# A two-dimensional spectral kernel: constants as weights along w, turns through DRAM and half-channel passes

## The chip, the cores and the metric

The kernel runs on one core of one Trainium2 chip. The metric is the device time of one execution in microseconds (us), the median of several runs. Engines are named as in the profile: PE (TensorE) multiplies, DVE (VectorE) and ACT (ScalarE) copy results out of PSUM and do the elementwise work, POOL (GpSimd) and SP (SyncE) issue DMAs. PEld is PE's load of weights.

## The reference

Four spectral layers follow one another on x of 2 x 64 x 64 x 384 in fp32 (batch, h, w, channels). Layers 0, 2 and 3 have this form:

```python
xs = jnp.fft.rfft2(x, axes=(1, 2))                 # 64 x 33 modes
o1r = relu(xr @ w1[0] - xi @ w1[1] + b1[0])        # 8 blocks of 48 channels
o1i = relu(xi @ w1[0] + xr @ w1[1] + b1[1])
o2r = o1r @ w2[0] - o1i @ w2[1] + b2[0]
o2i = o1i @ w2[0] + o1r @ w2[1] + b2[1]
out = jnp.fft.irfft2(softshrink(o2r) + 1j * softshrink(o2i)) + x
```

Layer 1 has a Hartley transform over the batch, h, w and channels in place of the FFT, the same kind of block product on all 64 by the first 33 of its modes (with the mirrored array beside it), and adds its result to its input too. Between layers nothing but this addition touches the array in space, so the kernel stays in the space of modes from the first layer to the last.

## The kernel before, in words

Work is cut into units. `order()` writes all of them out in one list, and every engine walks that list in order. A unit fills one of four PSUM units of two banks on PE, then ACT and DVE empty it; PE waits before unit n until unit n-4 is empty (`take`). Keys name the stage, the image and the place.

**First part, per image** (2 images, i). `S1` transforms along w: the pixels of two rows of h (128 partitions) by 128 channels are the weights, and the constant `dft_w`, which holds the two rows apart with zeros, streams (132 columns, L623). `T1` turns each of 33 modes and 3 channel tiles with a transpose (L645). Then come 20 rounds, one for each step: a step is 6 or 7 modes of w (`GROUPS`) by a pair of the 8 channel blocks. A round holds `S2` (transform along h, L657), `TA` of step n-4 (transposes back, L688), `S3` of step n-1 and `S4` of step n-2 (the two block products, L669 and L678). `S3` uses 48 of 64 rows in the two row halves, `S4` the two 64-column halves. On DVE `S4` is shrunk (L1087) and added to the modes (L1073 or L1076); POOL stores the sum in the DRAM array `spectrum`. After the 20 rounds comes the inverse, only to get the flipped array that layer 1 wants: `5A` along h with the modes as weights (L704), `2A` transposes (L715), `6A` along w (L725), then a store to `flipped`. Image 1 begins after that.

**Middle part** (10 items of modes and image): `CF`, `H1`, `H2`, `CI` do layer 1 (L747 to L784), from `spectrum`, its channel-mirrored copy `mirrored` (made by DMA, L480) and `flipped`. The result goes to `update` and `update_mirrored`.

**Last part, per image**: 20 rounds plus 3 of `3L2`, `3L3`, `4L2`, `4L3`, `TC`: two layers' products in the same lines L669 and L678, and the transposes L688. DVE joins the loaded update to step n+2 in between. Then `5C` (L704), `2C` (L715) and `6C`: PSUM is split into a high and a low fp32r part on ACT and DVE (L1276) and three one-pass products of 512 columns give the output (L736). Image 1 follows.

S1, for one of these:

```python
for k in range(min(2 * S1_BANK, HP - 2 * S1_BANK * u)):
    at = k // S1_BANK * BANK + k % S1_BANK * n
    mm = nc.tensor.matmul(bank[:, at:at + n], X[:, 2 * S1_BANK * u + k, t * P:(t + 1) * P], dft_w,
                          start=True, stop=True)
```

SP's queue issues loads and the mirror copies, POOL's the stores, each in its own order; a DMA behind a wait on SP is late with all that follows.

## Time and profile before

| | |
|---|---|
| median of 3 runs | 1116.82 us (1116.59 to 1116.85) |
| the profiled execution | 1116.76 us, span of the core 1114.9 us, mean granted clock 0.979 |
| PE, DVE, ACT, POOL busy | 1059.5, 570.9, 513.4, 107.9 us |
| share of PE in the chain of waits | 88% |
| moved by DMA | 117.94 MB, mean 106 GB/s |

Busy time is that of instructions on the engine. An fp32 matmul stands as two records, one after the other; a transpose as one. The chain of waits is the work that ended last, followed back from the end; in order of time it says which stage the kernel stands in. The granted clock is 1 at 2.4 GHz.

### The profile page before, as it was taken

To read this page: it belongs to the slowest core of one execution; us is meant where nothing else is said; L and a number is where in the kernel's file an instruction comes from. 1 tells how busy PE (TensorE), PEld (TensorE's weight loads), DVE (VectorE), ACT (ScalarE), POOL (GpSimd) and SP (SyncE) were. 2 spreads that over 40 slices of the span, in tenths; PEclk is the share of its full clock that TensorE was granted. 3 is DMA by queue.
4 is the path that set the end of the run, shared out by engine and by line. 5 is a ranking of instruction groups with operands and counts; after the bars stand their busy time and mean duration, and the time that the engine had idled before them with its cause. 6 is when DMAs were issued, how large, how long until landed. Compare 5 with 4: busy or idle time off the path is not lost.

```text
span 1114.9 us, 15851 instructions
## 1 busy us (share of the span) xinstructions
PE 1059.5 (95%) x6238; PEld 657.1 (59%) x6238; DVE 570.9 (51%) x893; ACT 513.4 (46%) x783; POOL 107.9 (10%) x160
## 2 busy tenths in 40 slices
PE   5899999999999999999999998899998989999896
PEld 5865569997555895444444444244446954444495
DVE  2645565344555552451424222477775567777645
ACT  2355553345555332422233231266665546666544
POOL 0011220000112100001111112100000120000003
PEclk9899999999999999999999998699999989999999
DMA  9713331100333595445345632543330184330016
GB/s 307 261 30 83 97 101 44 79 40 25 83 87 100 137 270 161 77 112 112 108 98 151 123 107 73 153 112 86 86 100 14 57 226 105 89 86 22 2 39 188
DMA packets 108058, 117.94 MB, mean 106 GB/s; under 512 B 69302, under 2 KB 93478, under 8 KB 107218
## 3 DMA queue, kind: packets, MB, share of 16 engines
q1 hardware_dynamic: 84626, 68.91, 24.4%
q0 software_dynamic: 22048, 45.99, 13.8%
q10 hardware_dynamic: 1312, 2.03, 0.6%
q8 instruction: 51, 0.84, 0.3%
q14 instruction: 21, 0.17, 0.1%
HBM read 77.41 MB, written 52.25 MB: 116 GB/s over the span
## 4 chain that ended last, share of the span: by engine, by line
PE 88%; DVE 5%; issue 3%; ACT 2%; DMA 1%; POOL 0%; SPq 0%; ACTq 0%; DVEq 0%
PE psum L678 16%; PE psum L669 15%; PE psum L784 8%; PE psum L747 8%; PE psum L704 8%; PE psum L657 6%; PE psum L761 5%; PE psum L688 4%; PE psum L623 4%; PE psum L725 4%; PE psum L715 4%; PE psum L736 3%; PE psum L772 3%; PE psum L645 2%; DVE RA L1087 1%
## 5 line engine op out<-in xcount | busy, mean ns | idle before, releaser
L1087 DVE SCALAR_TENSOR_TENSOR RA<-psum,RA 112x896 f32<-112x896 f32 (+1 forms) x120 | 124.3, 1036 | 196.7 <-ACT RA L922 196.7
L1049 DVE COPY RD<-psum 128x396 f32<-128x396 f32 (+5 forms) x110 | 73.1, 667 | 175.5 <-PE psum L747 91.1
L922 ACT ACTIVATE RA<-psum,small 112x896 f32<-112x896 f32 (+1 forms) x120 | 115.7, 964 | 82.3 <-PE psum L678 81.3
L678 PE MATMUL psum<-RA,RW 112*64 112x448 f32 (+1 forms) x640 | 135.7, 546 | 10.2 <-ACT RA L913 5.4
L899 ACT ACTIVATE RD<-psum 128x396 f32<-128x396 f32 (+7 forms) x106 | 60.8, 574 | 156.5 <-PE psum L747 67.1
L913 ACT ACTIVATE RA<-psum,RW 112x448 f32<-112x448 f32 (+1 forms) x160 | 89.2, 609 | 91.4 <-PE psum L669 91.4
L899 ACT ACTIVATE RB<-psum 128x512 f32<-128x512 f32 (+1 forms) x128 | 73.1, 571 | 104.4 <-PE psum L704 69.0
L1049 DVE COPY RB<-psum 128x512 f32<-128x512 f32 (+1 forms) x130 | 84.7, 653 | 70.7 <-PE psum L704 53.4
L704 PE MATMUL psum<-const,RD 128*128 128x128 f32 (+1 forms) x792 | 93.5, 279 | 4.9 <-DVE RD L1049 3.5
L678 PEld LDWEIGHTS psum<-RA,RW 112*64 112x64 f32 x640 | 40.3, 139 | 96.6 <-issue 67.5
L704 PEld LDWEIGHTS psum<-const,RD 128*128 128x128 f32 x792 | 91.5, 195 | 8.4 <-DVE RD L1049 3.9
L784 PE MATMUL psum<-RB,RD 112*128 112x448 f32 (+1 forms) x240 | 92.1, 537 | 3.1 <-DVE RB L1238 3.1
L747 PE MATMUL psum<-RX,RD 128*112 128x448 f32 (+1 forms) x240 | 89.9, 525 | 0.0
L1073 DVE TENSOR_TENSOR RX<-RX,RA 112x768 f32<-112x768 f32 (+2 forms) x80 | 80.7, 1009 | 1.4
L669 PE MATMUL psum<-RX,RW 48*112 48x448 f32 (+1 forms) x320 | 71.2, 566 | 4.4 <-DVE RX L1076 2.3
L784 PEld LDWEIGHTS psum<-RB,RD 112*128 112x128 f32 x240 | 46.3, 197 | 47.1 <-issue 36.0
L657 PEld LDWEIGHTS psum<-const,RB 128*112 128x112 f32 x528 | 59.7, 177 | 24.2 <-ACT RA L913 21.5
L899 ACT ACTIVATE RA<-psum 112x896 f32<-112x896 f32 (+2 forms) x64 | 44.3, 693 | 55.4 <-PE psum L725 29.0
L747 PEld LDWEIGHTS psum<-RX,RD 128*112 128x112 f32 x240 | 40.9, 177 | 47.2 <-issue 33.8
L678 PE MATMUL psum<-RA,RB 112*64 112x448 f32 (+1 forms) x320 | 64.0, 520 | 5.0 <-ACT RA L913 5.0
L657 PE MATMUL psum<-const,RB 128*112 128x128 f32 x528 | 67.1, 279 | 0.0
L669 PE MATMUL psum<-RA,RW 48*112 48x448 f32 (+1 forms) x320 | 67.0, 537 | 0.0
(91 smaller groups left out, 1329.7 us busy)
## 6 DMA issues: line engine op xcount, KB each, us to landing
out<-RB POOLq DMA_DIRECT2D x24, 512.0 KB, 3.8
RX<-x SPq DMA_DIRECT2D x10, 1152.0 KB, 13.5
spectrum<-RA POOLq DMA_DIRECT2D x48, 168.0 KB, 2.8
RX<-spectrum SPq DMA_DIRECT2D x48, 168.0 KB, 3.3
flipped<-RA POOLq DMA_DIRECT2D x6, 1056.0 KB, 4.8
spectrum<-RA POOLq DMA_DIRECT2D x32, 144.0 KB, 2.6
RX<-spectrum SPq DMA_DIRECT2D x32, 144.0 KB, 2.9
mirrored<-spectrum SPq DMA_DIRECT2D x6, 672.0 KB
```

What stands on the lines that cost most here:

```text
L657: mm = nc.tensor.matmul(bank[0:ROWS, k * P:(k + 1) * P], Bpair[:, k0 + k, g], dft_h, start=True, stop=True)
L669: mm = nc.tensor.matmul(dst, w3[layer][rows, a, g], src[rows, :, a], start=a == 0, stop=a == 1)
L678: mm = nc.tensor.matmul(bank[b * HALF:(b + 1) * HALF, a * BANK:a * BANK + nk * H], w4[layer][0:ROWS, g, b, a], hidden(slot)[0:ROWS, b * N: ...
L704: mm = nc.tensor.matmul(bank[:, at:at + n], D[:, k, t * P:(t + 1) * P], rhs, start=True, stop=True)
L747: mm = nc.tensor.matmul(bank[0:ROWS, half * BANK:half * BANK + n], fwd_c_view[:, t, 2 * h + half], y(q, 1 + 2 * b)[:, t], start=t == 0, st ...
L784: mm = nc.tensor.matmul(bank[:, half * BANK:half * BANK + n], inv_c_view[0:ROWS, g, t * P:(t + 1) * P], s_sum[b][0:ROWS, g, 0:n], start=g ...
L899: return nc.scalar.activation(dst, src, ACT.Copy)
L913: done = nc.scalar.activation(hidden(slot)[0:ROWS, b * N:b * N + nk * H], banks(key)[0:ROWS, b, 0:nk * H], ACT.Relu, bias=bias[layer][0:RO ...
L922: nc.scalar.activation(dst, src, ACT.Relu, bias=minus_lambda_l0 if key[0] == "S4" else minus_lambda).then_inc(act_emptied, 1)
L1049: return nc.vector.tensor_copy(dst, src)
L1073: last = nc.vector.tensor_tensor(m[:, :, k], m[:, :, k], src[:, :, k], ALU.add)
L1087: nc.vector.scalar_tensor_tensor(out=dst, in0=src, scalar=LAMBDA / 64 if key[0] == "S4" else LAMBDA, in1=dst, op0=ALU.add, op1=ALU.min).th ...
```

## The change

1. **Passes.** Images go through in four passes p of 192 channels (image p // 2, half p % 2). Steps are numbered s = 0 to 39 over both images, 10 to a pass; e = s // 2 numbers the 20 groups of modes. One list of rounds r runs over all 40 steps, in the first part as in the last: no pass ends before the next begins.
2. **Along w.** `S1` has the constant as weights (64 x 64) and x as the streaming side: four matmuls of 384 columns, one in each quarter of the array. `6C` is built alike, with plain fp32 and no split; so the `2C` units, L1276 and `inv_w_parts` go.
3. **Turns.** `T1`, `2A` and `2C` go. SP stores the transform along w to the DRAM array `rows_along_w` and loads it back with h on the partitions (`load_bm`); the inverse along h goes to `rows_along_h` (`store_turned`) and comes back with w's modes on the partitions (`load_g`).
4. **Along h, inverse.** `5A` and `5C` have the constant as weights and stream two modes of 192 channels.
5. `6A` works on 96 channels at a time. Preparing layer 1's operands on DVE is spread over steps 2 to 7. The `CF` units of the first two items go ahead of the `6A` units of the last pass.

On PE and in the plan:

```diff
--- before.py
+++ after.py
-            def s1(i, u, t):
-                key = ("S1", i, u, t)
-                if t == 0:
-                    pe.wait_ge(x_loaded[u], 16 * (i + 1))
+            def s1(p, v):
+                key, k = ("S1", p, v), v // 2
+                if v % 2 == 0:
+                    pe.wait_ge(x_loaded[k], 32 * (p + 1))
                 bank = take(key)
-                n = 4 * KW
-                for k in range(min(2 * S1_BANK, HP - 2 * S1_BANK * u)):
-                    at = k // S1_BANK * BANK + k % S1_BANK * n
-                    mm = nc.tensor.matmul(bank[:, at:at + n], X[:, 2 * S1_BANK * u + k, t * P:(t + 1) * P], dft_w,
-                                          start=True, stop=True)
+                n = 2 * PASS_C
+                for to in range(2):
+                    at = (to * X_HP // 2 + v % 2 * 2) * PASS_C
+                    for j in range(2):
+                        rows = slice(j * HALF, (j + 1) * HALF)
+                        mm = nc.tensor.matmul(bank[to * HALF:(to + 1) * HALF, j * BANK:j * BANK + n], dft_w[rows],
+                                              X(k)[rows, at:at + n], start=True, stop=True)
                 mm.then_inc(filled, 1)
...
-            def t1(i, v):
-                key = ("T1", i, v)
-                if v == 0:
-                    for t in range(NT):
-                        for u in (S1_UNITS - 2, S1_UNITS - 1):
-                            wait_emptied(pe, ("S1", i, u, t))
+            def s2(s):
+                key, e = ("S2", s), s // PASS_PAIRS
+                _, g, k0, nk = step_of(s)
                 bank = take(key)
-                for k in range(2 * v, min(2 * v + 2, KW)):
-                    for t in range(NT):
-                        at = (k % 2) * BANK + t * P
-                        mm = nc.tensor.transpose(bank[:, at:at + P], A(t)[:, :, k], identity)
-                mm.then_inc(filled, 1)
-
-            def s2(i, n):
-                key = ("S2", i, n)
-                q, g, k0, nk = step_of(n)
-                bank = take(key)
-                if g == 0:
-                    last = (k0 + nk - 1) // 2
-                    for v in (last - 1, last):
-                        wait_emptied(pe, ("T1", i, v))
+                if s == 0:
+                    pe.wait_ge(consts_loaded, 16)
+                if s % PASS_PAIRS == 0:
+                    wait_bm_loaded(pe, e)
+                cols = slice(g % PASS_PAIRS * ROWS, (g % PASS_PAIRS + 1) * ROWS)
                 for k in range(nk):
-                    mm = nc.tensor.matmul(bank[0:ROWS, k * P:(k + 1) * P], Bpair[:, k0 + k, g], dft_h,
+                    rows = slice(0, H) if k0 + k in (0, KW - 1) else slice(0, P)
+                    mm = nc.tensor.matmul(bank[0:ROWS, k * P:(k + 1) * P], Bm(e)[rows, k, cols], dft_h[rows],
                                           start=True, stop=True)
                 mm.then_inc(filled, 1)
...
-            def s5(key, matrix, turned):
-                _, i, t, u = key
-                if t == 0:
-                    modes = [k for m in inverse_banks(u) for k in bank_modes(m)]
-                    n = max(n for n in range(STEPS) if step_of(n)[1] == PAIRS - 1 and step_of(n)[2] <= max(modes))
-                    wait_emptied(pe, (turned, i, n))
+            def s5(key, matrix, stage, first):
+                _, e, part = key
+                if part == 0:
+                    for s in (PASS_PAIRS * e, PASS_PAIRS * e + 1):
+                        wait_emptied(pe, (stage, s))
                 bank = take(key)
-                for half, m in enumerate(inverse_banks(u)):
-                    at = half * BANK
-                    for k in bank_modes(m):
-                        rhs = matrix[:, 2 * H:3 * H] if k in (0, KW - 1) else matrix[:, 0:2 * H]
-                        n = rhs.shape[1]
-                        mm = nc.tensor.matmul(bank[:, at:at + n], D[:, k, t * P:(t + 1) * P], rhs, start=True, stop=True)
-                        at += n
+                for half in range(2):
+                    lo, hi = bank_modes(e, part, half)
+                    n = (hi - lo) * PASS_C
+                    dst = bank[:, half * BANK:half * BANK + n].rearrange("p (k c) -> p k c", c=PASS_C)
+                    mm = nc.tensor.matmul(dst, matrix, D(first + e)[:, lo:hi], start=True, stop=True)
                 mm.then_inc(filled, 1)
 
-            def t2(key, s5_stage):
-                _, i, t, v = key
-                if v == 0:
-                    for u in range(INV_UNITS):
-                        wait_emptied(pe, (s5_stage, i, t, u))
+            def s6a(key):
+                _, p, g, v = key
+                if g == 0 and v == 0:
+                    pe.wait_ge(g_loaded[p % 2], 32 * (p // 2 + 1))
                 bank = take(key)
-                for k in range(HP_UNIT):
-                    mm = nc.tensor.transpose(bank[:, k * P:(k + 1) * P], E(t)[:, :, v * HP_UNIT + k], identity)
-                mm.then_inc(filled, 1)
-
-            def s6a(key):
-                _, i, t, v = key
-                bank = take(key)
-                wait_emptied(pe, ("2A", i, t, v))
-                n = 2 * KW
-                for k in range(HP_UNIT):
-                    at = k // (HP_UNIT // 2) * BANK + k % (HP_UNIT // 2) * n
-                    mm = nc.tensor.matmul(bank[:, at:at + n], G(t, v)[:, k * P:(k + 1) * P], inv_w_flip,
+                n, cols = 2 * KW, slice(g * PASS_C // 2, (g + 1) * PASS_C // 2)
+                for k in range(FLIP_HP):
+                    at = k // (FLIP_HP // 2) * BANK + k % (FLIP_HP // 2) * n
+                    mm = nc.tensor.matmul(bank[0:PASS_C // 2, at:at + n], G(p)[:, v * FLIP_HP + k, cols], inv_w_flip,
                                           start=True, stop=True)
                 mm.then_inc(filled, 1)
 
             def s6c(key):
-                _, i, t, v = key
+                _, p, v = key
+                if v == 0:
+                    pe.wait_ge(g_loaded[p % 2], 32 * ((PASSES + p) // 2 + 1))
                 bank = take(key)
-                wait_emptied(pe, ("2C", i, t, v))
-                for half in range(2):
-                    cols = slice(half * BANK, (half + 1) * BANK)
-                    for n, (matrix, g) in enumerate(((0, 0), (1, 0), (0, 1))):
-                        mm = nc.tensor.matmul(bank[:, cols], inv_w_parts[:, matrix], split(t, v)[g][:, cols],
-                                              start=n == 0, stop=n == 2)
+                n, k = 2 * PASS_C, v // 2
+                for to in range(2):
+                    h = k * X_HP + to * X_HP // 2 + v % 2 * 2
+                    for j in range(2):
+                        rows = slice(j * HALF, (j + 1) * HALF)
+                        dst = bank[to * HALF:(to + 1) * HALF, j * BANK:j * BANK + n].rearrange("p (h c) -> p h c", c=PASS_C)
+                        mm = nc.tensor.matmul(dst, inv_w[rows], G(p)[rows, h:h + 2], start=True, stop=True)
                 mm.then_inc(filled, 1)
 
```

The first part's and last part's rounds, and SP's queue:

```diff
+def first_transform_round(p):
+    return 3 if p == 1 else 10 * p - 8
+
+
+def flip_round(p):
+    return 10 * p + 17
+
+
+def last_inverse_round(p):
+    return 10 * p + 16
+
+
+def order():
+    o = [("S1", 0, v) for v in range(S1_UNITS)]
+    for r in range(A_ROUNDS):
+        if r < ALL_STEPS:
+            o += [("S2", r)]
+        if 0 <= r - 4 < ALL_STEPS:
+            o += [("TA", r - 4)]
+        for p in range(1, PASSES):
+            if 0 <= r - first_transform_round(p) < X_PARTS:
+                o += [("S1", p, 2 * (r - first_transform_round(p)))]
+        for p in range(PASSES - 1):
+            if 0 <= r - flip_round(p) < FLIP_UNITS:
+                o += [("6A", p, 0, r - flip_round(p))]
+        if 0 <= r - 1 < ALL_STEPS:
+            o += [("S3", r - 1)]
+        if 0 <= r - 6 < 2 * ALL_GROUPS:
+            o += [("5A", (r - 6) // 2, (r - 6) % 2)]
+        if 0 <= r - 2 < ALL_STEPS:
+            o += [("S4", r - 2)]
+        for p in range(1, PASSES):
+            if 0 <= r - first_transform_round(p) < X_PARTS:
+                o += [("S1", p, 2 * (r - first_transform_round(p)) + 1)]
+        for p in range(PASSES - 1):
+            if 0 <= r - flip_round(p) < FLIP_UNITS:
+                o += [("6A", p, 1, r - flip_round(p))]
+        if r == PREP_ROUND:
...
+    for r in range(C_ROUNDS):
+        if r < ALL_STEPS:
+            o += [("3L2", r)]
+        if 0 <= r - L3_LAG - 3 < 2 * ALL_GROUPS:
+            o += [("5C", (r - L3_LAG - 3) // 2, (r - L3_LAG - 3) % 2)]
+        if 0 <= r - L3_LAG < ALL_STEPS:
+            o += [("3L3", r - L3_LAG)]
+        if r < ALL_STEPS:
+            o += [("4L2", r)]
+        for p in range(PASSES - 1):
+            if 0 <= r - last_inverse_round(p) < S1_UNITS:
+                o += [("6C", p, r - last_inverse_round(p))]
+        if 0 <= r - L3_LAG < ALL_STEPS:
+            o += [("4L3", r - L3_LAG)]
+        if 0 <= r - L3_LAG - 1 < ALL_STEPS:
+            o += [("TC", r - L3_LAG - 1)]
+    o += [("6C", PASSES - 1, v) for v in range(S1_UNITS)]
...
+            def store_stage(p, k):
+                wait_emptied(sp, ("S1", p, 2 * k))
+                wait_emptied(sp, ("S1", p, 2 * k + 1))
...
+                for to in range(2):
+                    at = (2 * k + to) * n
+                    sp.dma_start(dst[:, :, at:at + n], src[to * HALF:(to + 1) * HALF]
+                                 ).then_inc(stage_stored[(p * X_PARTS + k) % STAGE_SLOTS], 16)
+
+            def load_bm(e):
+                p, q, k0, nk = group_of(e)
+                if q == 0:
+                    for k in range(1, X_PARTS):
+                        wait_stage_stored(sp, p, k)
+                loaded = bm_loaded[e % BM_SLOTS]
+                src = rows_along_w[p].rearrange("q h r -> h q r")
+                n_re = nk - (q == PASS_GROUPS - 1)
...
+                sp.dma_start(Bm(e)[0:H, 0:n_re], src[:, 2 * k0:2 * (k0 + n_re):2]).then_inc(loaded, 16)
+                sp.dma_start(Bm(e)[H:P, skip:n_re], src[:, 2 * (k0 + skip) + 1:2 * (k0 + n_re):2]).then_inc(loaded, 16)
...
+            def store_turned(e):
+                p, q, k0, nk = group_of(e)
...
+                sp.dma_start(dst[:, 2 * k0:2 * (k0 + n_re):2], turned(e)[0:H, 0:n_re]).then_inc(stored, 16)
+                sp.dma_start(dst[:, 2 * (k0 + skip) + 1:2 * (k0 + n_re):2], turned(e)[H:P, skip:n_re]).then_inc(stored, 16)
...
+            def load_g(p):
+                for e in (PASS_GROUPS * (p + 1) - 2, PASS_GROUPS * (p + 1) - 1):
+                    wait_turned_stored(sp, e)
...
+                for j in range(2):
+                    sp.dma_start(G(p)[j * Q:(j + 1) * Q], rows_along_h[p, :, j * HP:(j + 1) * HP]
+                                 ).then_inc(g_loaded[p % 2], 16)
...
+            for r in range(A_ROUNDS):
+                for p in range(1, PASSES):
+                    k = r - first_transform_round(p)
+                    if 0 <= k < X_PARTS:
+                        store_stage(p, k)
+                        if p + 1 < PASSES:
+                            load_x(p + 1, k)
+                e = (r + 4) // 2
+                if r % 2 == 0 and BM_SLOTS <= e < ALL_GROUPS:
+                    wait_filled(sp, ("S2", 2 * (e - BM_SLOTS) + 1))
+                    load_bm(e)
+                if r % 2 == 1 and 0 <= (r - 7) // 2 < ALL_GROUPS:
+                    e = (r - 7) // 2
+                    for part in range(2):
+                        wait_emptied(sp, ("5A", e, part))
+                    store_turned(e)
+                for p in range(PASSES - 1):
+                    if r == 10 * p + 16:
+                        load_g(p)
+                for i in range(B):
+                    if r % 2 == 1 and 0 <= r - i * STEPS - 15 < 2 * PASS_GROUPS:
+                        mirror(i, (r - i * STEPS - 15) // 2)
```

**PE's order, the end of the first inverse.** Before, PE's rows at the end of image 0 (L704 is 5A, L688 TA, L715 2A, L725 6A, L623 S1):

```order
L688 MATMUL psum<-const,RA 128x112 x6
L678 MATMUL psum<-RA,RW 64x384 x4
L704 MATMUL psum<-const,RD 128x128 x8
L688 MATMUL psum<-const,RA 128x112 x6
L704 MATMUL psum<-const,RD 128x128 x8
```

And in the change, a round with transform units of pass 2 and the next ones (L825 is S2, L856 TA, L802 S1, L837 S3, L870 5A, L846 S4):

```order
L825 MATMUL psum<-const,RX 112x128 x7
L856 MATMUL psum<-const,RA 128x112 x7
L802 MATMUL psum<-RX,const 64x384 x4
L837 MATMUL psum<-RA,RW 112x448 x4
L870 MATMUL psum<-RD,const 128x192 x2
L846 MATMUL psum<-RA,RW 64x448 x4
L802 MATMUL psum<-RX,const 64x384 x4
```

The inverse along h (5A) and the transform of a later pass (S1) have moved into the rounds, between units that split the array.

**SP's order in the change, from the end of round 15 to the array of pass 0** (L529 is a staged store of pass 2, L517 x of pass 3, L552 to L555 the turned group 4, L591 a mirror copy, L541 and L542 a load for S2, L569 the array for 6A of pass 0):

```order
L529 DMA rows_along_w<-RX 128x1x896 [waits vec_emptied,act_emptied]
L529 DMA rows_along_w<-RX 128x1x896
L517 DMA RX<-x 64x8x192 x2
L552 DMA rows_along_h<-RD 64x5x192 [waits vec_emptied,act_emptied]
L553 DMA rows_along_h<-RD 64x5x192
L555 DMA rows_along_h<-RD 64x192
L591 DMA mirrored<-spectrum 7x384x64 [waits modes_stored3,modes_stored4,modes_stored1,modes_stored0]
L541 DMA RX<-rows_along_w 64x7x224 [waits stage_stored1,stage_stored2,stage_stored0,filled]
L542 DMA RX<-rows_along_w 64x6x224
L569 DMA RG<-rows_along_h 64x6144 [waits prep_stored,turned_stored0,turned_stored1]
L569 DMA RG<-rows_along_h 64x6144
```

All of these but the mirror copy and x are new, and the array for 6A comes last of them.

**The end of PE's list in the change** (L896 is 6C):

```order
L856 MATMUL psum<-const,RX 128x112 x6
L870 MATMUL psum<-RD,const 128x384 x2
L896 MATMUL psum<-RG,const 64x384 x4
L870 MATMUL psum<-RD,const 128x192 x2
L896 MATMUL psum<-RG,const 64x384 x32
```

The last eight units of 6C (x32) stand behind the last unit of 5C, with nothing between.

## Rows read from the trace of the kernel before

**Rows 1.** The page: busy time, share of the span and instructions by engine

```profile
PE 1059.5 (95%) x6238; PEld 657.1 (59%) x6238; DVE 570.9 (51%) x893; ACT 513.4 (46%) x783; POOL 107.9 (10%) x160
```

**Rows 2.** Chain of waits in order of time, first part: start us, us, what

```profile
45.13 12.41 PE psum L645 x99
57.54 3.06 PE psum L657 x28
...
101.05 1.71 PE psum L657 x14
...
106.78 1.71 PE psum L657 x14
...
171.75 11.43 PE psum L704 x100
183.18 3.60 PE psum L715 x32
...
194.14 1.74 PE psum L725 x16
...
222.57 21.67 PE psum L623 x192
```

**Rows 3.** The same view, middle and last part

```profile
559.46 4.05 PE psum L747 x12
...
891.75 1.40 PE psum L736 x6
...
939.67 0.82 PE psum L688 x7
...
946.85 0.82 PE psum L688 x7
```

**Rows 4.** Timeline of PE: start us, us, line, operation, out<-in, count [idle before]

```profile
171.75 10.48 PE L704 MATMUL psum<-const,RD 128*128 128x128 f32 x92 [1.73 <-DVE RD L1049]
...
818.87 1.51 PE L678 MATMUL psum<-RA,RW 112*64 112x384 f32 x8 [0.28 <-DVE RA L1087]
820.21 1.46 PE L678 MATMUL psum<-RA,RB 112*64 112x384 f32 x8
821.60 0.79 PE L688 MATMUL psum<-const,RX 112*128 112x112 f32 x6
822.33 1.55 PE L669 MATMUL psum<-RX,RW 48*112 48x384 f32 x8
...
854.01 0.74 PE L688 MATMUL psum<-const,RX 112*128 112x112 f32 x6
854.59 1.96 PE L704 MATMUL psum<-const,RD 128*128 128x128 f32 x16
...
857.87 11.43 PE L704 MATMUL psum<-const,RD 128*128 128x128 f32 x100 [0.74 <-ACT RD L899]
...
907.35 2.28 PE L669 MATMUL psum<-RX,RW 48*112 48x448 f32 x8 [2.26 <-DVE RX L1076]
```

**Rows 5.** Groups by line and form: count, busy us, mean ns, idle before

```profile
L704 PEld LDWEIGHTS psum<-const,RD 128*128 128x128 f32 x792 | 91.5, 195 | 8.4 <-DVE RD L1049 3.9 <-ACT RD L899 1.9 <-DVE RA L1087 1.2
L657 PEld LDWEIGHTS psum<-const,RB 128*112 128x112 f32 x528 | 59.7, 177 | 24.2 <-ACT RA L913 21.5 <-issue 2.7
L1049 DVE COPY RB<-psum 128x384 f32<-128x384 f32 x34 | 18.7, 555 | 7.9 <-PE psum L645 7.9
```

**Rows 6.** Stretches (engines busy, PEclk, DMA share, GB/s) and a DMA issue

```profile
57.50:172.00 114.50, 112.77 (x751) 68.48 (x750) 61.20 (x104) 60.47 (x83) 22.52 (x45) 1.00 0.32 81
375.00:400.00 25.00, 25.00 (x222) 25.00 (x222) 10.52 (x16) 9.06 (x16) 0.00 (x0) 0.98 0.92 217
400.00:425.00 25.00, 25.00 (x220) 24.53 (x220) 15.10 (x22) 8.47 (x18) 1.11 (x2) 1.00 0.84 263
700.00:725.00 25.00, 21.07 (x68) 7.35 (x70) 11.56 (x37) 8.16 (x12) 3.49 (x3) 0.66 0.56 165
...
spectrum<-RA POOLq DMA_DIRECT2D x48, 168.0 KB, 2.8
```

938 lines of the change are left out of this document (496 added, 442 removed).

## The prediction

> **What bounds the kernel now.** I read the page first. PE is busy for 1059.5 of 1114.9 us, and nothing else is above 51% [rows 1]. So a change pays if it takes matmuls away or fills PE's 55 us of idleness; what it gives VectorE, ScalarE or the DMA queues costs only where PE comes to wait for it. The chain of waits in order of time gives every stage its length: each fp32 matmul is two records there, so x192 is 96 matmuls. In the first part [rows 2] a step of the mode rounds takes 5.73 us (101.05 to 106.78) and the stages along w and the inverse stand apart from the rounds. In the last part [rows 3] a round takes 7.18 us (939.67 to 946.85). The timeline [rows 4] prices matmuls that share the array, and the lines by form [rows 5] the weight loads. The stretches and DMA issues [rows 6] say what a turn through DRAM costs. The sum is made against the profiled execution, 1116.8 us with its 1.9 us around the span; the median of the runs is the same.
>
> **Matmul work taken out.** From the two chains [rows 2, 3]: the transform along w, 21.67 us per image, 43.3; its transposes, 12.41 each, 24.8; the inverse along h, 11.43 us per 100 records for 792 of them, 90.5; the 192 transposes of each inverse, 3.60 us per 32 records for 384 in all, 43.2; the flipped inverse along w, 1.74 per 16 for 384, 41.8; the last inverse, 24 units of 1.40, 33.6. Together 277.
>
> **Matmul work put in.** (a) The transform along w and the last inverse become 32 units each of four fp32 matmuls of 384 columns, one in each array quarter, so 8 records a unit. No row shows four quarters at once. Two 64-column halves at once take 1.34 us for 8 records of 384 columns (818.87 to 820.21) [rows 4], and the whole array takes 4.05 us for 12 [rows 3], 2.7 us for 8: a half doubles the rate and nothing of it is lost. Bounds for a unit are thus 0.70 us (doubled again) and 1.39 us (halves only; the spacing of 820.21 to 821.60). I take 0.70, because both row halves and column halves pair up fully in this kernel: 64 x 0.70 = 45 us. (b) The inverse along h gets the constant as its weights and 160 matmuls of 384 or 192 columns instead of 396 of at most 128: 208 records at 4.05/12 = 0.34 and 112 at some 0.18 give 90 us, the same as before. Fewer weight loads gain nothing, since streaming already set the pace. (c) The flipped inverse goes from 192 to 256 matmuls of 66 columns. They are bound by the load of the weights: 0.109 us a record is twice what 66 columns stream in. The weights have 96 columns instead of 128, and loads shrink with columns (195 against 177 ns for 128 and 112) [rows 5]. Between 0.082 and 0.109 us a record I take 0.082: 42 us. (d) Switching between whole and split array: six transposes before another whole-array matmul take 0.58 us (854.01 to 854.59), before a split one 0.73 (821.60 to 822.33) [rows 4]. The 80 inverse units now stand between row-split and column-split products, 0.15 us each, and the quarter units add about 0.05 to 0.1 each: 16 us. Together 193, and the net is **277 - 193 = 84 us less**.
>
> The Trainium skill (TensorEngine Tiling (Array Packing), § Key Properties) says that four 64x64 tiles run independently, and that changing the tiling mode drains the engine. By the first a unit takes 0.70 us as in my sum. By the second each switch would cost more than my row shows; the trace agrees that a switch costs something, 0.15 us.
>
> **Evacuation.** A quarter unit is copied out by two engines, 384 columns each. VectorE takes 555 ns for such a copy [rows 5], less than the 0.70 us of the unit, and two such units share a round with others; VectorE's 61 us in the 114.5 us of the first rounds [rows 6] leave room. I cost it at nothing in the first part. In the last part a round puts seven units through four PSUM units where five went before, and the copy of a last-inverse unit stands behind shrink, join and add; PE needs that PSUM unit four units later. Without that cover it is up to 1 us a round; I take 0.1, 4 us in all.
>
> **Turns through DRAM: the new waits.** At full share the queues move 263/0.84 = 313 GB/s, and a single 168 KB store lands after 2.8 us, so some 2.2 us are latency [rows 6]. Per pass of 192 channels an array for the inverse along w is 3.15 MB, 10.1 us. PE reaches that inverse (6A) about one and a half to two rounds after the last 5A unit of the pass, which is 9 to 11 us later, while on SP's queue stand, for pass 0: the last staged store 2.9, the next part of x 2.5, the turned store 2.2, the mirror copy 3.2, a load for the forward transform 2.5, then the array 10.1 and latency 2.2, and 2 for the mode stores beside them: 27.7 us against 9.3, so PE stands for **18 us**. For pass 1 there is no x and no mirror: 22 against 9.3, **13**. Pass 2: 20 against 11, **9**. Pass 3: 18 against the 7 us of three CF units, **11**. Each stop also lets the clock fall (the granted clock was 0.66 in the 25 us after the quiet stretch at 700 us [rows 6]): 2 us each, 8. Together **59 us**. The mirror's 3.2 us are what is left of the DMA share 0.32 over 114.5 us after 6.5 MB of mode stores, by five mirrors. In the last part the same chain takes about 13.5 us from the end of round 10p+14 and PE arrives 14 us after it: no wait for three passes. For the last pass nothing is left to cover it: copy 0.6, store 2.2, latency 2.2, array 10.1, latency 2.2, and 3 for the clock: **20 us**. What the ring holds is then late next: every load for the forward transform has four rounds of slack, so I cost those at nothing; if the queue runs behind by more than that they are a rival.
>
> The Trainium skill (DMA: Bandwidth & Descriptors, § Why a DMA increments its semaphore by 16 and not by 1) says that a copy whose slowest dimension is 7 uses 7 engines. The mirror copies are 7x384x64, so by it the first stop would be some 4 us longer, and that of pass 2 too.
>
> **Start.** Before, the first S2 starts at 57.54, with 35.8 us of PE work ahead of it, 22 idle. Now x (3.15 MB) and constants (1.3 MB), the stores of all four staged parts (3.7 MB), each at 313 GB/s, latency 2.2 twice and one load 2.5 plus 2.2 give about 35 us, with 5.6 us of work: 29.5 idle, **+8**.
>
> **Waits that go.** The last part restarted for image 2: 2.3 us idle before 907.35 [rows 4], then 32.3 us to the first transpose at 939.67 [rows 3] for 19.2 us of work, so 15.4. Each image's inverse began with a wait, 1.73 us before 171.75 in the first part and 0.74 before 857.87 in the last [rows 4], twice each, 5. And 3 of some 6 us that PE lost to VectorE's joins in the six-mode rounds (0.28 before 818.87 is the smallest of them [rows 4]). **-23**.
>
> **Sum.** -84 + 4 + 59 + 20 + 8 - 23 = -16 us; 1116.8 - 16 = **1101 us**, with 1075 to 1118 as this case's own range. A run tells 0.2% (2.2 us) from no change.
>
> **Rivals.**
> 1. *The quarters run only two at a time* (slower). For: rows show only two sharing the array. Against: it loses nothing in either direction. A unit is then 1.39 us, 64 x 0.69 = 44 us more: 1145. It ends slower than before as soon as a unit takes over 0.95 us (16 us over 64 units).
> 2. *The round trips are hidden*: the transfers start earlier or run nearer full speed than I think, and stops last 3 us each: 1101 - 45 = 1056. For: all stops are differences of two estimates of 10 to 28 us. Against: the array can't be asked for before the last turned group is in DRAM.
> 3. *The first part becomes DMA-bound* (slower). Some 98 MB move in it by the shapes, at 313 GB/s 313 us of about 430. In the rounds with a transform unit x, staged store, turned store, forward load and modes ask for 8.5 us of an 8.3 us round. If small pieces take the rate down to 217/0.92 = 236 GB/s, as between 375 and 400 us before [rows 6], the queue falls behind and each of the four stops grows by 10: 1141.
> 4. *Switches cost more*: at 0.5 us each instead of 0.15 the 16 us become 53: 1138. This is the mechanism by which the skill's rule on drains would decide.
> 5. *It does not do what it says*, gaining and paying the same: within 2 us of 1116.8.
>
> **Chances.** Forecast 0.42, rival 2 0.20, rival 1 0.15, rival 3 0.10, rival 4 0.08, rival 5 0.05. Faster: 0.42 and 0.20, less what of the forecast's edge is slower, 0.61; same 0.05; slower 0.34. The range that leaves out 2 in 10 goes from 1050 (just below rival 2) to 1145 (rival 1).
>
> **What would show it.** S1 and 6C groups with PE starts 0.70 us apart per unit (1.39 is rival 1); the 5A group at about 90 us with 5C; PE idle just before the first unit of each 6A pass, released by a DMA into RG, 18, 13, 9 and 11 us, and once some 17 before the last eight 6C units; S2 first at 35 us; PE busy 84 us less in the chain. I am wrong if idle is spread through the rounds with VectorE or a forward load as releaser, or if the stops are below 5 us.

## The result and the profile after

The changed kernel takes 1245.24 us (median of 4 runs, 1241.03 to 1257.93) against 1116.70 in the runs of before beside it: a ratio of 1.119, 95% interval 1.114 to 1.124. It is slower by 129 us where I forecast 16 us less, and it lies outside the range. The profiled execution took 1248.62 us, with a span of 1246.4.

First the page: the busy line, the granted clock in 40 slices, the shares of the chain and the DMA traffic. [Rows 1] holds the busy line of before.

```profile
PE 1018.5 (82%) x5296; PEld 511.5 (41%) x5296; DVE 514.2 (41%) x856; ACT 472.2 (38%) x747; POOL 127.2 (10%) x203
...
PEclk8899967995899788589999999799998998998986
...
DMA packets 174855, 197.41 MB, mean 158 GB/s; under 512 B 73639, under 2 KB 155159, under 8 KB 172995
...
PE 68%; DMA 17%; SPq 6%; issue 3%; DVE 3%; ACT 2%; POOL 1%; ACTq 0%; DVEq 0%; POOLq 0%
```

PE is busy 41.0 us less, but the span is 131.5 us longer: PE stands idle for 227.9 us where it was 55.4. The clock line has five dents that before had not, and DMA and SP's queue now hold 23% of the chain. The waits of PE (line, releaser: us in total, times, longest) say where:

```profile
PE psum L881 <- DMA RG<-rows_along_h: 109.4, 4, 31.2
PE psum L896 <- DMA RG<-rows_along_h: 43.7, 4, 26.3
PE psum L825 <- DMA RX<-rows_along_w: 17.3, 1, 17.3
```

Below, a trip is the way of one pass's array through DRAM, and a stop is PE's idle time before the inverse that needs it. L881 is the flipped inverse along w (6A), L896 the last inverse (6C), RG the array they read. The turns through DRAM cost 153.1 us of idle, 31.1, 30.8, 16.3 and 31.2 before 6A and 5.8, 6.7, 4.9 and 26.3 before 6C; I had 51 and 17. The chain in order of time shows the first of these stops (start us, us, what):

```profile
155.05 8.37 DMA rows_along_w<-RX
...
163.50 7.81 SPq L541
...
172.69 18.84 DMA RG<-rows_along_h
...
191.57 2.83 PE psum L881 x16
```

PE had run out of work at 160.5. In this first stop three things stand one behind the other: a staged store that takes 8.37 us to land, the issue of a forward load (L541) that holds SP's queue for 7.81 us, and the array, 18.84 us from issue to landing. SP's own timeline shows what stood ahead of that long issue: the mirror copy (L591), from DRAM to DRAM.

```profile
162.18 1.06 SPq L591 DMA_DIRECT2D mirrored<-spectrum  x1
163.50 7.81 SPq L541 DMA_DIRECT2D RX<-rows_along_w  x1
...
172.10 1.19 SPq L569 DMA_DIRECT2D RG<-rows_along_h  x2
```

The stretches (us, then PE, PEld, DVE, ACT, POOL busy, granted clock, DMA share, GB/s) of three stops and of the work right behind them:

```profile
160.50:191.60 31.10, 0.03 (x1) 0.03 (x1) 1.91 (x3) 0.21 (x1) 1.00 (x2) 0.54 0.91 213
191.60:200.30 8.70, 8.70 (x32) 5.27 (x34) 0.96 (x2) 2.15 (x4) 0.00 (x0) 0.50 0.00 0
...
485.20:516.40 31.20, 0.01 (x2) 0.01 (x1) 0.62 (x1) 0.54 (x1) 0.00 (x0) 0.58 0.88 203
516.40:541.60 25.20, 25.20 (x140) 22.55 (x142) 4.83 (x8) 6.09 (x10) 1.03 (x2) 0.50 0.20 59
937.00:942.80 5.80, 0.03 (x2) 0.00 (x0) 3.10 (x8) 0.90 (x1) 0.00 (x0) 0.85 0.91 192
942.80:947.90 5.10, 5.06 (x19) 1.47 (x20) 0.56 (x1) 0.71 (x2) 0.00 (x0) 0.51 0.71 199
```

Behind a stop PE works at the lower level (0.50, 1.2 GHz): 8.7 us behind the first, 25.2 behind the fourth, 5.1 behind the first of 6C. Over all eight stops such work takes 73 us; by an estimate that takes half of it for lost, the clock costs 36. In the stops shown the DMA engines are at 0.88 to 0.91, but move only 192 to 213 GB/s.

The groups of the quarter units by form (count, busy us, mean ns, idle before) and the timeline of PE inside a round:

```profile
L896 PE MATMUL psum<-RG,const 64*64 64x384 f32 x256 | 30.7, 575 | 43.7 <-DMA RG<-rows_along_h 43.7
...
L802 PE MATMUL psum<-RX,const 64*64 64x384 f32 x256 | 29.2, 541 | 11.1 <-DMA RX<-x 11.1
```

```profile
148.78 1.72 PE L846 MATMUL psum<-RA,RW 112*64 112x448 f32 x8
150.44 0.88 PE L802 MATMUL psum<-RX,const 64*64 64x384 f32 x8
151.24 1.56 PE L825 MATMUL psum<-const,RX 128*112 128x128 f32 x12
```

A unit of eight records in array quarters (L802) takes 0.80 us from start to the next start, a switch on either side included. Two at a time would be 1.39, so the quarters run more than two at once; two runs at the end price the products alone.

### The profile page after: what moved, and what is told of

Read it like the earlier page. It is cut to its first block, busy times and chain, and to the rows that moved or that the text cites. A ratio compares the mean times of both kernels' runs of the same rounds, so it can differ in the third digit from the quotient of the medians.

```text
span 1246.4 us, 14444 instructions
## 1 busy us (share of the span) xinstructions
PE 1018.5 (82%) x5296; PEld 511.5 (41%) x5296; DVE 514.2 (41%) x856; ACT 472.2 (38%) x747; POOL 127.2 (10%) x203
## 3 DMA queue, kind: packets, MB, share of 16 engines
q0 software_dynamic: 22720, 45.99, 12.4%
## 4 chain that ended last, share of the span: by engine, by line
PE 68%; DMA 17%; SPq 6%; issue 3%; DVE 3%; ACT 2%; POOL 1%; ACTq 0%; DVEq 0%; POOLq 0%
PE psum L837 13%; PE psum L846 12%; DMA RG<-rows_along_h 12%; PE psum L945 7%; PE psum L870 7%; PE psum L906 6%; PE psum L922 5%; PE psum L825 5%; PE psum L881 4%; PE psum L856 3%; PE psum L933 3%; DMA rows_along_h<-RD 2%; DMA rows_along_w<-RX 2%; PE psum L802 2%; SPq L599 2%
## 5 line engine op out<-in xcount | busy, mean ns | idle before, releaser
L881 PE MATMUL psum<-const,RG 128*96 128x66 f32 x512 | 61.6, 290 | 109.4 <-DMA RG<-rows_along_h 109.4
L846 PE MATMUL psum<-RA,RW 112*64 112x448 f32 (+1 forms) x640 | 136.1, 547 | 2.7 <-ACT RA L1086 2.7
L870 PE MATMUL psum<-RD,const 128*128 128x384 f32 (+1 forms) x320 | 110.7, 471 | 9.5 <-DVE RA L1194 6.1
L1080 ACT ACTIVATE RA<-psum 128x384 f32<-128x384 f32 (+3 forms) x82 | 55.8, 680 | 159.8 <-PE psum L945 56.8
L881 PEld LDWEIGHTS psum<-const,RG 128*96 128x96 f32 x512 | 58.7, 204 | 118.5 <-DMA RG<-rows_along_h 110.8
L1194 DVE COPY RD<-psum 128x672 f32<-128x672 f32 (+2 forms) x120 | 68.7, 573 | 88.0 <-PE psum L870 74.7
L945 PE MATMUL psum<-RG 112*128 112x448 f32 (+1 forms) x240 | 90.6, 530 | 3.1 <-DVE RG L1396 3.1
L906 PE MATMUL psum<-RX,RF 128*112 128x448 f32 (+1 forms) x240 | 90.6, 529 | 0.5 <-DVE RD L1194 0.5
L870 PEld LDWEIGHTS psum<-RD,const 128*128 128x128 f32 x320 | 55.5, 196 | 75.0 <-issue 31.2
L825 PE MATMUL psum<-const,RX 128*112 128x128 f32 (+1 forms) x528 | 71.9, 285 | 17.3 <-DMA RX<-rows_along_w 17.3
L1080 ACT ACTIVATE RD<-psum 128x384 f32<-128x384 f32 (+2 forms) x120 | 64.3, 536 | 52.9 <-PE psum L870 36.6
L825 PEld LDWEIGHTS psum<-const,RX 128*112 128x112 f32 (+1 forms) x528 | 62.0, 180 | 37.8 <-issue 34.8
L1080 ACT ACTIVATE RN<-psum 96x264 f32<-96x264 f32 x32 | 19.9, 623 | 150.3 <-PE psum L881 150.3
L837 PE MATMUL psum<-RA,RW 48*112 48x448 f32 (+1 forms) x320 | 71.1, 564 | 4.0 <-ACT RX L1080 2.1
L846 PEld LDWEIGHTS psum<-RA,RW 112*64 112x64 f32 x640 | 40.1, 140 | 81.5 <-issue 75.3
```

Source lines behind the costliest of these rows:

```text
L825: mm = nc.tensor.matmul(bank[0:ROWS, k * P:(k + 1) * P], Bm(e)[rows, k, cols], dft_h[rows], start=True, stop=True)
L837: mm = nc.tensor.matmul(dst, w3[layer][rows, a, g], src[rows, :, a], start=a == 0, stop=a == 1)
L846: mm = nc.tensor.matmul(bank[b * HALF:(b + 1) * HALF, a * BANK:a * BANK + nk * H], w4[layer][0:ROWS, g, b, a], hidden(slot)[0:ROWS, b * N: ...
L870: mm = nc.tensor.matmul(dst, matrix, D(first + e)[:, lo:hi], start=True, stop=True)
L881: mm = nc.tensor.matmul(bank[0:PASS_C // 2, at:at + n], G(p)[:, v * FLIP_HP + k, cols], inv_w_flip, start=True, stop=True)
L906: mm = nc.tensor.matmul(bank[0:ROWS, half * BANK:half * BANK + n], fwd_c_view[:, t, 2 * h + half], y(q, 1 + 2 * b)[:, t], start=t == 0, st ...
```

## The experiments

The theory after this reading: the matmul sum is about right, and the loss lies in the trips of the array. It is made of (1) the load into half of the partitions, (2) the queue behind the mirror copies, (3) the clock behind each stop. Its rival: the first part is bound by its transfers as a whole, so that a wait removed comes back in the rounds.

**Mirror copies behind the array loads.** `mirror(0, q)` moves from rounds 15, 17, ... to 17 to 21, after `load_g(0)`; those of image 2 to rounds 37 and 38 and behind `load_g(3)`.

```
-                    if r % 2 == 1 and 0 <= r - i * STEPS - 15 < 2 * PASS_GROUPS:
-                        mirror(i, (r - i * STEPS - 15) // 2)
+                    if 0 <= r - i * STEPS - 17 < (PASS_GROUPS, 2)[i]:
+                        mirror(i, r - i * STEPS - 17)
...
             load_g(PASSES - 1)
+            for q in range(2, PASS_GROUPS):
+                mirror(1, q)
```

> The mirror copies (SP, DRAM to DRAM) are moved behind the array loads. Theory A, the queue: each of them holds the next DMA issue on SP by some 7.5 us (7.81, 7.54, 8.47 us in the trace of the change), so the stops before the inverse along w of passes 0 and 3 shrink from 31 to about 23 us, that of pass 1 from 31 to about 27; idle time falls by some 20 us and the half-clock time behind it a little: about 1220 us. Rival B, transfers: the queue would have waited for the turned stores and for the engines anyway, and the stops stay within 3 us of 31, 31, 16, 31: about 1243 us.

Measured 1221.32 us (ratio 1.097, 1.091 to 1.103), 24 us less. The waits of PE:

```profile
PE psum L883 <- DMA RG<-rows_along_h: 80.0, 4, 25.6
PE psum L898 <- DMA RG<-rows_along_h: 44.0, 4, 26.5
```

The four stops before 6A are 25.6, 22.8, 11.8 and 19.9 us, 29.4 us less together; the waits of 6C, which has no mirrors, are the same. That the long issue belongs to the copy ahead of it is shown by where it goes. The forward load of the first stop is now issued in 0.59 us, and the same kind of load behind the first moved copy holds the queue for 6.85:

```profile
165.25 0.59 SPq L541 DMA_DIRECT2D RX<-rows_along_w  x1
...
198.87 6.85 SPq L541 DMA_DIRECT2D RX<-rows_along_w  x1
```

So theory A holds, though the first stop lost 5.5 us and not 7.8. Why the issue takes so long isn't shown.

**The inverse along w three rounds later.**

```
 def flip_round(p):
-    return 10 * p + 17
+    return 10 * p + 20
```

(The load of the middle part's weights, which waits for 6A of pass 2, goes from round 41 to 44.)

> The inverse along w of passes 0 to 2 is done three rounds later (three rounds are about 25 us), everything else as in the change. Theory A, latency of the trip alone: the stops of 31, 31 and 16 us before these three passes go (78 us of idle), and with them the half clock behind each, about 10 us a time: about 1245 - 78 - 30 = 1137 us, with the stop of pass 3 still 31. Rival B, the first part is bound by the transfers: PE then waits as long in the rounds, for forward loads or staged parts, and at most a third of it is won: 1205 to 1240 us.

Measured 1200.85 us (1.078, 1.073 to 1.083): 44 us less, between the two expectations, at the edge of the rival's. Waits of PE, and SP's queue from 245 us:

```profile
PE psum L881 <- DMA RG<-rows_along_h: 45.7, 3, 30.6
...
PE psum L825 <- DMA RX<-rows_along_w: 24.5, 2, 16.8
...
PE psum L856 <- issue: 8.5, 1, 8.5
```

```profile
245.51 3.31 SPq L591 DMA_DIRECT2D mirrored<-spectrum  x1
248.98 16.49 SPq L529 DMA_DIRECT2D rows_along_w<-RX  x2
265.51 2.40 SPq L541 DMA_DIRECT2D RX<-rows_along_w  x1
```

Three rounds were 20 us, too few for 31: pass 0 still waits 12.0 us, pass 1 3.1, pass 2 none. Two new waits took the place of a part of what was won: 7.7 us before an S2 and 8.5 before a TA. The first is the queue again: two staged stores take 16.49 us to issue behind a mirror, and the forward load behind them comes late. That is the rival in part.

**One DMA over 128 partitions.** This run loads the rows in another order of partitions, so 6A and 6C work on permuted data; amounts and shapes are those of the change.

```
-                for j in range(2):
-                    sp.dma_start(G(p)[j * Q:(j + 1) * Q], rows_along_h[p, :, j * HP:(j + 1) * HP]
-                                 ).then_inc(g_loaded[p % 2], 16)
+                sp.dma_start(G(p), rows_along_h[p].rearrange("q (j h) c -> (q j) h c", j=2)
+                             ).then_inc(g_loaded[p % 2], 16)
```

> The 3.15 MB array of a pass comes in one DMA over all 128 partitions, 24 KB each, instead of two of 64 partitions; the rows land in another order of partitions, so this run does not compute the inverse along w of the right data. Theory A, a DMA into half of the partitions has about two thirds of the rate (213 against 313 GB/s): the load takes 10 us instead of 15, all eight trips are 5 us shorter, with the first-half part of the clock some 50 us together, less where a stop is only 5 us: about 1205 us. Rival B, the rate is set by the memory side or by what else is in flight: landing stays at 17 to 19 us, and the time at 1245 us.

Measured 1184.61 us (1.063, 1.058 to 1.068): 61 us less, more than expected. With nothing else in flight, in the last trip, the stretch of this run and, below, of the change:

```profile
1155.00:1162.00 7.00, 0.00 (x0) 0.00 (x0) 0.00 (x0) 0.00 (x0) 0.00 (x0) 0.50 0.88 379
```

```profile
1211.00:1226.00 15.00, 0.00 (x0) 0.00 (x0) 0.00 (x0) 0.00 (x0) 0.00 (x0) 0.50 0.89 184
```

379 GB/s against 184 at the same busy share. The load lands after 10.1 us there and the pair after 18.1 (issued at 1208.54, landed at 1226.59). The three short stops of 6C are gone but for 0.2 us, and the last is 18.3 us. For the expectation I had taken 213 against 313 GB/s; the measured rates lie further apart.

**Two DMAs of 64 partitions, each from a contiguous 1.57 MB.** It separates the partitions reached from the pattern in DRAM; the data are permuted as above.

```
+                rows = rows_along_h[p].rearrange("q (j h) c -> (q j) h c", j=2)
                 for j in range(2):
-                    sp.dma_start(G(p)[j * Q:(j + 1) * Q], rows_along_h[p, :, j * HP:(j + 1) * HP]
+                    sp.dma_start(G(p)[j * Q:(j + 1) * Q], rows[j * Q:(j + 1) * Q]
```

> Two DMAs of 64 partitions as in the change, but each reads one contiguous 1.57 MB of DRAM instead of every other 24 KB; rows land in another order, so the data of the inverse along w are not the right ones. Theory A, the number of partitions reached sets the rate: each DMA still takes about 7 us to stream, the pair lands 17 to 19 us after its issue, 1245 us. Rival B, the strided source or the pattern in DRAM set it: the pair lands in 12 us as the single DMA did, 1185 us.

Measured 1249.67 us (1.124, 1.117 to 1.131); last trip:

```profile
1216.00:1230.00 14.00, 0.00 (x0) 0.00 (x0) 0.00 (x0) 0.00 (x0) 0.00 (x0) 0.50 0.95 197
```

Nothing is won, so the pattern of the source isn't the cause. This run and the one before differ in the number of partitions, and also in the number of DMAs, two against one. The best version below settles that: there the array comes as four DMAs, each into all 128 partitions, and while they are in flight, with stores to `out` beside them, the queues move 369 GB/s:

```profile
1059.00:1065.00 6.00, 1.65 (x12) 0.80 (x16) 0.00 (x0) 0.00 (x0) 3.27 (x6) 0.60 0.98 369
```

It is the 64 partitions.

**The upper half on POOL's queue**, so that the two halves are in flight at once (`pool.dma_start(G(p)[Q:P], ...)` with semaphores of its own).

> Two DMAs of 64 partitions as in the change, but the one for the upper half of the partitions is issued on the queue of POOL, so that both halves are in flight at the same time. Theory A, each half of the partitions has a rate of its own (some 220 GB/s) and the two rings are served in turn: both land within 12 us of the later issue, and the time comes near that of the single DMA over 128 partitions, 1185 to 1200 us. Rival B, two transfers aren't fused even so, as the engines work through one after the other: the later lands 17 to 19 us after the issue, and the time stays at 1240 to 1250 us.

Measured 1238.79 us (1.111, 1.105 to 1.118); last trip:

```profile
1201.00:1216.00 15.00, 0.00 (x0) 0.00 (x0) 0.00 (x0) 0.00 (x0) 0.00 (x0) 0.50 0.88 184
```

The halves were issued at 1198.54 and 1199.02 and landed after 14.1 and 17.3 us, so both were in flight. The rate is 184 GB/s again: two transfers into different halves don't add up, not even from two queues. The Trainium skill (SBUF — State Buffer, § Door 1: The DMA port swizzle) says that partitions 0 to 63 reach 8 of 16 ports, an asymptote of about 218 GB/s against 436, and that two DMAs on the two halves serialize. The traces agree: 184, 197 and 184 GB/s in the last trips of the change and of the two runs into halves, against 379. My prediction had not weighed this page.

**The right layout.** `rows_along_h` is laid out (pass, j, q, h, c), so that one DMA brings every row to its place; each turned store is split in two, of 32 partitions.

```
-        rows_along_h = dram("rows_along_h", (2 * PASSES, Q, H, PASS_C))
+        rows_along_h = dram("rows_along_h", (2 * PASSES, 2, Q, HP, PASS_C))
...
+                for j in range(2):
+                    dst = rows_along_h[p, j].rearrange("q h c -> h q c")
+                    re, im = slice(j * HP, (j + 1) * HP), slice(H + j * HP, H + (j + 1) * HP)
...
+                sp.dma_start(G(p), rows_along_h[p].rearrange("j q h c -> (j q) h c")
```

> The scratch array in DRAM is laid out half of h first, so that the 3.15 MB of a pass come in one DMA over 128 partitions into the right places; each turned store becomes two, of 32 partitions each, instead of one of 64. Theory A, what held the trips was the load into 64 partitions: it takes 12 us instead of 19 as in the run with the other order of partitions, and the gain of that run, 60 us, comes but for 1 to 2 us a trip for the doubled stores: 1185 to 1200 us. Rival B, DMAs with 32 partitions as source run at half the rate of those with 64: some 1.5 us more for each of 40 turned stores, on the queue of the first part: 1205 to 1220 us.

Measured 1184.95 us (1.067, 1.060 to 1.073), the same as with permuted data: what the doubled stores cost is below what these runs tell apart.

**PE kept busy in the stops.** 30, 30, 14, 30 and 5, 6, 4, 26 fp32 products of 512 columns before the waits for the array, into the PSUM unit that is overwritten next.

```
                 bank = take(key)
                 if g == 0 and v == 0:
+                    keep_busy(bank, "6A", p)
                     pe.wait_ge(g_loaded[p % 2], 32 * (p // 2 + 1))
```

> PE is given matmuls to do, into the PSUM unit it holds, through nearly all of each of the eight stops (30, 30, 14, 30 and 5, 6, 4, 26 fp32 products of 512 columns, 0.9 us each at full clock); their results are overwritten. Theory A, the clock: the stops keep their length, but PE leaves them at full clock instead of working at half clock for some 15 to 20 us, which costs about 8 us behind each of the five long ones: 1245 - 40 to 50 = about 1200 us. Rival B, what my forecast had, 2 us a stop: about 1232 us or, as the filling may run over the end of a stop, no change.

Measured 1244.30 us (1.116, 1.111 to 1.121), no change, which is the rival's number. But PE still stood before the array had landed, 5.2, 1.9, 4.7 and 5.8 us before 6A (below, the rest behind the first filling, then the work behind it):

```profile
188.00:193.20 5.20, 0.02 (x1) 0.02 (x1) 0.00 (x0) 0.00 (x0) 0.00 (x0) 0.98 0.68 137
193.20:203.20 10.00, 10.00 (x34) 5.62 (x36) 0.97 (x2) 2.16 (x4) 0.00 (x0) 0.50 0.01 4
```

5.2 us of rest, and the next 10.0 us ran at the lower level as if the whole stop had been idle. So this run doesn't decide between clock and rival. The next fills the stops to their ends: 37, 34, 20, 38 and 8, 9, 6, 32 products.

> As the run before with PE kept busy in the stops, but with more products, so that they end after the array has landed: 37, 34, 20, 38 before the inverse along w of passes 0 to 3 and 8, 9, 6, 32 before the last inverse of passes 0 to 3. In the shorter filling PE still stood 5.2, 1.9, 4.7 and 5.8 us before the first four and worked at half speed behind them all the same. Theory A, any idle of a few us sets the clock back: now it stays full, and the 75 us that PE worked at the lower level behind the eight stops take half the time, -37 us; the overrun of the filling adds some 14: about 1222 us. Rival B, the filling isn't what holds the clock, or the short products of the inverse along w don't: half speed as before behind the stops, 1245 to 1258 us.

Measured 1222.40 us (1.100, 1.092 to 1.107), 23 us less. The stretches behind the first and the fourth stop:

```profile
194.00:204.00 10.00, 10.00 (x77) 6.99 (x75) 3.75 (x6) 4.62 (x7) 0.38 (x1) 1.00 0.30 72
...
510.40:521.40 11.00, 11.00 (x129) 10.87 (x127) 4.25 (x7) 4.36 (x7) 0.52 (x1) 1.00 0.24 74
```

The clock is full throughout, and the 6A of the fourth pass takes 11.0 us for its 128 records where the change took 20.7. So the theory of the clock holds. That the time met the 1222 expected is luck in part: I had put the overrun of the filling at 14 us, but from first product to last the eight fillings take 158.8 us where the stops took 153.1, 5.7 more. The half of the 73 us (36) less 5.7 would have gained 31; 23 came, and the other 8 I can't place. The clock is thus worth some 29 to 36 us of the 129.

**All remedies at once**: the layout; the array in four DMAs by range of h with a semaphore each; mirrors behind the loads; 6A of passes 0 to 2 three rounds later, that of pass 3 behind the first products of the middle part; 6C of pass 2 moved into the last trip.

> All remedies at once: DRAM layout for 128 partitions and the array in four DMAs by range of h, each with its own semaphore; mirror copies behind the array loads; the inverse along w of passes 0 to 2 three rounds later, that of pass 3 behind the first products of the middle part; the last inverse of pass 2 moved into the last trip. If the stops are trips, and these end as measured (12 us of load, 7.5 us of queue), the four stops of the first part go (109 us of idle) with some 25 us of half clock behind them, the three short ones of the last part too (17 idle and 9 of clock), and the last shrinks from 26 to some 8 us: 1245 - 109 - 25 - 26 - 18 = about 1067 us. Rival: the first part is then bound by its transfers, about 20 us an image: 1105 us.

Measured 1098.70 us (0.988, 0.983 to 0.992): 1.2% below before, clear of the interval. It is 32 us above the 1067 expected and near the rival's 1105; the waits of PE show 23 of the 32:

```profile
PE psum L832 <- DMA RX<-rows_along_w: 20.3, 2, 15.7
PE psum L929 <- DMA RG<-flipped: 11.8, 1, 11.8
...
PE psum L903 <- DMA RG<-rows_along_h: 9.2, 4, 5.9
PE psum L863 <- issue: 6.5, 1, 6.5
```

A forward load was 4.6 us late, the flipped rows of pass 3 11.8, and a TA waited 6.5. The other 9 us I can't place.

**The best version.** 6A of pass 2 two rounds earlier, and the forward transform `CF` of item 2 of the middle part ahead of the Hartley product that waited. The edit is against the run before:

```
 def flip_round(p):
-    return 10 * p + 20
+    return 10 * p + (18 if p == 2 else 20)
...
     for z in range(ITEMS + 2):
+        if z == 1:
+            o += [("CF", 2, 0), ("CF", 2, 1)]
```

> All remedies, and two changes to the order that the trace of that run suggests: the inverse along w of pass 2 two rounds earlier, since its array landed 13 to 19 us before it was used, and the products of the second forward transform of the middle part in front of the Hartley product that stood 11.8 us for the flipped rows of pass 3. Theory A, stops are trips not covered: the 11.8 us wait shrinks to some 2 us and half of the 6.3 us of half clock behind it goes: 1098.7 - 12 = 1087 us. Rival B, the transfers of that stretch are on the queue of SP and the wait only moves to the loads for the next products: 1096 to 1099 us.

Measured 1085.76 us (0.974, 0.969 to 0.979) of 6 runs, against 1115.77 of before in the same rounds: 2.6% faster than before, and 13% faster than the change it is made of. As theory A had it, the wait for the flipped rows fell from 11.8 to 2.9 us. Its page and waits:

```profile
PE 992.1 (91%) x5296; PEld 496.5 (46%) x5296; DVE 512.2 (47%) x856; ACT 472.6 (44%) x747; POOL 127.3 (12%) x203
```

```profile
PE psum L834 <- DMA RX<-rows_along_w: 19.6, 2, 15.6
PE psum L905 <- DMA RG<-rows_along_h: 11.3, 4, 8.5
```

**The units' products twice, then the inverse's.** Two runs on the best version price the new matmuls. In the first the four products of each of the 64 quarter units are issued twice with the same result, in the second the products of each of the 80 units of the inverse along h.

```
-                for to in range(2):
+                for to in (0, 1, 0, 1):
...
-                for half in range(2):
+                for half in (0, 1, 0, 1):
```

> On the best version, each of the 64 units of the transform along w and of the last inverse issues its four products twice, with the same result. Theory A, the quarters run four at once: a unit's products cost 0.64 to 0.70 us more, 64 times 41 to 45 us: about 1129 us. Rival B, they run two at a time (1.39 us a unit): +89, 1175 us. What lies above 0.70 in the units' measured 0.87 us is then the switch to and from split array, which isn't paid twice.

> On the best version, each of the 80 units of the inverse along h issues its products twice. Theory A, my forecast's 90 us are the products' own time and the 10 us that the trace shows above it are paid for switching: +90 us, 1176 us. Rival B, the products themselves are slower than the 0.34 and 0.18 us a record that I took: +100 us or more, 1186 us.

Measured 1099.27 us (0.985, 0.980 to 0.991), some 13 us more, and 1150.65 (1.032, 1.026 to 1.037), some 65 more: below every expectation. The groups of the best version, of the units twice and of the inverse twice:

```profile
L879 PE MATMUL psum<-RD,const 128*128 128x384 f32 x208 | 83.7, 515 | 9.5 <-DVE RA L1203 5.0 <-DVE RD L1203 2.3 <-ACT RD L1089 1.8
...
L890 PE MATMUL psum<-const,RG 128*96 128x66 f32 x512 | 48.1, 249 | 0.0
...
L811 PE MATMUL psum<-RX,const 64*64 64x384 f32 x256 | 32.4, 595 | 9.7 <-DMA RX<-x 9.7
L905 PE MATMUL psum<-RG,const 64*64 64x384 f32 x256 | 27.1, 526 | 11.3 <-DMA RG<-rows_along_h 11.3
L879 PE MATMUL psum<-RD,const 128*128 128x192 f32 x112 | 26.0, 337 | 1.0 <-DVE RA L1203 1.0
```

```profile
L811 PE MATMUL psum<-RX,const 64*64 64x384 f32 x512 | 49.5, 513 | 7.9 <-DMA RX<-x 7.9
...
L905 PE MATMUL psum<-RG,const 64*64 64x384 f32 x512 | 47.0, 503 | 2.6 <-DMA RG<-rows_along_h 2.6
```

```profile
L879 PE MATMUL psum<-RD,const 128*128 128x384 f32 x416 | 154.7, 501 | 7.8 <-DVE RA L1203 5.0 <-ACT RD L1089 1.8 <-DVE RD L1203 0.6
...
L879 PE MATMUL psum<-RD,const 128*128 128x192 f32 x224 | 48.2, 332 | 1.0 <-DVE RA L1203 1.0
```

Busy time of the units rises by 37.0 us (96.5 less 59.5), 0.58 a unit: below my 0.70. Two at a time is excluded (89). In a round a unit takes 0.80 us from start to start, so the way into and out of the split array is 0.22. The 59.5 us of the group are 0.93 a unit, because records overlap their neighbours and some units run at the lower level behind a wait.

The groups of the inverse rise by 93.2 us (202.9 less 109.7), PE's busy time as a whole by 79.8 (1071.9 less 992.1), since neighbouring records overlap. So the products cost 80 to 93 us where I forecast 90, and by the groups some 16 us, 0.2 a unit, are paid once for switching.

The time rises less than the work. In the profiled executions PE is busy 42.5 us more with the units twice and the span is 21.5 longer, since PE's idle time falls from 92.8 to 71.8; with the inverse twice it falls by 14.0. The longer rounds cover waits that stood in the shorter ones: those before 6C (L905) fall from 11.3 to 2.6 us. (The profiled execution with the units twice, 1108.23, lies above the median of its runs.) That gap between work and time is the lesson on the best version: it is no longer bound by matmuls alone.

## Why the prediction was wrong

The forecast was busy -73 us (-84 work, +11 clock) and idle +57 (51 and 17 in stops, 8 at the start, 4 for evacuation, less 23). Measured: busy -41.0, idle +172.5. The step that failed first and cost most is the price of the load of the array, then the price of the mirror copy on the queue, then the clock behind a stop.

- **Matmul work, 84 us less**: held in the main. At the mean granted clock of before (0.979 in both) the best version's PE is busy 992.1 us against 1059.5, 67 less. The quarters run four at once (0.58 us of products a unit). A unit takes 0.80 us from start to start, so 64 of them 51 us where I had 45 and 3 to 6 for switches. 6A's group is 48.1 us for 42 forecast, its overlaps counted. A switch costs about 0.2 us by both runs that issue products twice, not 0.5. So rivals 1, 4 and 5 fell, and rival 2 with the stops.
- **The array at 313 GB/s, 10.1 us**: the step that failed first. I took the rate from a mixed stretch of [rows 6], whose transfers reach 112 or 128 partitions but for the loads of flipped rows at its end, and scaled it by the busy share; the changed load goes into 64 at a time. The array took 17.3 to 19.0 us from issue to landing where I had 12.3, in each of eight trips. Replacing it alone gave 61 us.
- **"The mirror copy 3.2"**: the second. I priced its share of the DMA engines, not its hold on the queue. Issues behind a mirror took 7.8 us in the first stop and 8.5 in the fourth; moving the copies gave 24 us. The rule of the Trainium skill that the prediction cites (DMA: Bandwidth & Descriptors, § Why a DMA increments its semaphore by 16 and not by 1: a copy whose slowest dimension is 7 uses 7 engines, by my estimate "some 4 us longer") pointed this way, and I took the value without it. How many engines the copies used no run here shows.
- **Latency 2.2 us**: holds only where the queue is quiet. With 313 GB/s it gives 3.7 us for a staged store of 448 KB and 3.3 for a turned store of 336 KB; their medians are 7.4 and 5.0, and the staged store ahead of the first stop took 8.4.
- **"2 us each" for the clock**: the third. It was 4 to 5 us behind the first three stops, 12.6 behind the fourth and 2 to 3 behind each of those of 6C, 36 in all by that estimate for 11 forecast; the longer filling won back at least 23 of it.
- **"No wait for three passes"** in the last part: 5.8, 6.7 and 4.9 us, all from the load's rate, gone with one DMA of 128 partitions. The last trip: 26.3 for 17, and 18.3 with one DMA.
- **Waits that go, -23**: failed. The 15.4 us at the restart for image 2 weren't idle. In the kernel before, PE has 5 us of gaps there and works some of it at the lower level (0.50 from 910 to 915 us); I had also left matmuls out of my 19.2 us. VectorE's waits moved to other lines instead of going.
- **Start, +8**: the moment held, S2 first starts at 36.6 us (35 forecast). The idle time did not: it is 28.4 us against 16.0 before, 12.4 more. My 22 us before was partly work at less than full pace, the same slip as at the restart.
- **Rival 3** (the queue falls behind, each stop 10 us longer, 1141) was the nearest, and named place and direction, but for another reason, small pieces; the cause was the number of partitions. The stops grew by 7 to 20 us and not by 10.
- **Rival 2's price**, 45 us, isn't the sum of its own terms: stops of 51 and 17 us cut to five of 3 us give 53, which would put that rival at 1048 us and not at 1056.

What stays open: I didn't try what the staged and x transfers, also 64 partitions at a time, would gain over 128; and the 17 us between the 84 forecast and the 67 measured of matmul work are told by groups only in part. Why an issue behind a mirror copy takes so long is open too.

## What to carry to other kernels

Price a transfer by the partitions it reaches, not by the rate of the busiest stretch, and lay out scratch arrays in DRAM so that each load covers all 128; two DMAs into the halves don't add up. A round trip through DRAM costs its latency on a loaded queue, everything ahead of it on that queue (a DRAM-to-DRAM copy of 2,688 rows of 256 bytes held the next issue for 7 to 8.5 us here), and the clock behind the stop, so ask what PE can do in it before moving work through DRAM. A change whose matmul gain is real can lose all of it to eight waits, and some 30 changed lines turned +11.9% into -2.6%.
